# Raw attention slabs split inside each attention, logits turned, opening by tiles, one head's scores a slot later

## The reference

```python
x = x + 0.5 * ffn(layernorm(x))
x = x + attn(layernorm(x))
x = x + 0.5 * ffn(layernorm(x))
```

## Time and profile before

| what | value |
|---|---|
| median of three executions | 1925.19 us (1920.02 to 1925.96) |
| the profiled execution, its own time | 1923.59 us |
| its span, first to last instruction | 1921.9 us |
| PE busy | 1871.7 us (97%) |
| DVE busy | 781.9 us (41%) |
| ACT busy | 507.0 us (26%) |
| POOL busy | 134.1 us (7%) |
| granted TensorE clock, mean | 0.996 of 2.4 GHz |

### The profile page before, as it was taken

How to read it: one execution, slowest core, us unless ns; L and a number is a source line. 1 busy time by engine, 2 the same in 40 slices (tenths; PEclk the granted TensorE clock), 3 DMA queues, 4 the chain that set the end, 5 groups by cost and what they waited for, 6 DMA issues and landing times.

```text
span 1921.9 us, 23031 instructions
## 1 busy us (share of the span) xinstructions
PE 1871.7 (97%) x9024; PEld 1564.9 (81%) x9024; DVE 781.9 (41%) x1464; ACT 507.0 (26%) x780; POOL 134.1 (7%) x231
## 2 busy tenths in 40 slices
PE   4899999999999999999999999999999999999998
PEld 3778787888888888888888888888888888888887
DVE  4456644454343454323424455343454323423222
ACT  2333421343213332111311343213332111311111
POOL 0012110010000100000001010000100000000000
PEclk9899999999999999999999999999999999999999
DMA  4798876555575644576567564575644576567664
GB/s 146 250 352 330 296 285 255 191 191 170 174 249 186 211 165 165 193 242 230 203 222 271 192 216 171 170 249 186 211 165 165 195 245 233 198 220 253 222 238 162
DMA packets 95099, 416.38 MB, mean 217 GB/s; under 512 B 11760, under 2 KB 12144, under 8 KB 67984
## 3 DMA queue, kind: packets, MB, share of 16 engines
q1 hardware_dynamic: 56416, 291.29, 42.6%
q0 software_dynamic: 12336, 77.34, 10.3%
q10 hardware_dynamic: 26240, 46.28, 8.9%
HBM read 365.71 MB, written 49.15 MB: 216 GB/s over the span
## 4 chain that ended last, share of the span: by engine, by line
PE 91%; DVE 3%; ACT 2%; DMA 2%; issue 1%; SPq 1%; ACTq 0%; DVEq 0%
PE bank L932 26%; PE bank L934 26%; PE bank L933 26%; PE bank L1153 4%; PE bank L942 1%; PE bank L964 1%; PE bank L963 1%; PE bank L1082 1%; PE bank L1096 1%; DMA wt<-scr_w 1%; PE bank L1095 1%; PE bank L1088 1%; DMA b_all<-wgu 1%; DVE act_t L608 1%; PE bank L987 0%
## 5 line engine op out<-in xcount | busy, mean ns | idle before, releaser
L932 PE MATMUL bank<-x_hi,wt 128*128 128x512 f32 x1408 | 558.2, 396 | 4.1 <-DMA wt<-scr_w 2.7
L934 PE MATMUL bank<-x_lo,wt 128*128 128x512 f32 x1408 | 550.8, 391 | 0.0
L933 PE MATMUL bank<-x_hi,wt 128*128 128x512 f32 x1408 | 550.4, 391 | 0.0
L608 DVE TENSOR_TENSOR act_t<-bank,sig 128x512 f32<-128x512 f32 x176 | 121.6, 691 | 645.7 <-PE bank L1153 636.5
L932 PEld LDWEIGHTS bank<-x_hi,wt 128*128 128x128 f32 x1408 | 265.8, 189 | 57.5 <-DMA wt<-scr_w 3.6
L934 PEld LDWEIGHTS bank<-x_lo,wt 128*128 128x128 f32 x1408 | 265.3, 188 | 57.1
L933 PEld LDWEIGHTS bank<-x_hi,wt 128*128 128x128 f32 x1408 | 265.7, 189 | 52.3
L932 PE MATMUL bank<-dt,a_hi 128*128 128x512 f32 x704 | 279.5, 397 | 0.3 <-DVE a_lo L608 0.3
L934 PE MATMUL bank<-dt,a_hi 128*128 128x512 f32 x704 | 275.1, 391 | 0.0
L933 PE MATMUL bank<-dt,a_lo 128*128 128x512 f32 x704 | 274.3, 390 | 0.0
L561 ACT ACTIVATE sig<-bank 128x512 f32<-128x512 f32 x176 | 105.3, 598 | 503.2 <-PE bank L1153 503.2
(11 more groups left out here) (166 smaller groups left out, 1752.0 us busy)
## 6 DMA issues: line engine op xcount, KB each, us to landing
wt<-scr_w SPq DMA_DIRECT2D x154, 1152.0 KB, 5.2
dt<-scr_d SPq DMA_DIRECT2D x154, 512.0 KB, 5.2
s_bc<-scr_s ACTq DMA_DIRECT2D x128, 256.0 KB, 5.3
tw<-scr_t POOLq DMA_DIRECT2D x28, 1024.0 KB, 5.3
scr_w<-wt POOLq DMA_DIRECT2D x22, 1152.0 KB, 8.4
b_all<-wgu SPq DMA_DIRECT2D x22, 512.0 KB, 7.6
scr_d<-dt POOLq DMA_DIRECT2D x22, 512.0 KB, 6.1
scr_t<-tw POOLq DMA_DIRECT2D x7, 1024.0 KB, 7.7
```

The lines of the kernel that those rows point to most:

```text
L608: return nc.vector.tensor_tensor(dst, a, b, op)
L932: mm(dst, wh, xh, start=start, stop=False)
L933: mm(dst, wl, xh, start=False, stop=False)
L934: return mm(dst, wh, xl, start=False, stop=stop)
```

## The change

It removes the scratch copy of the attention slabs (scr_t, store_t, raw_slab, the splits in phase 0). Each attention now loads the raw slab (512 KB, POOL's queue) into raw_t, which becomes the state tile, and ACT and DVE split it in the slots of SPLIT. PE waits for the split (t_lo_ok) where it waited for the load. Besides: the logits are made the other way round (gate_s stationary, 512 tokens moving: 8 matmuls), copied whole by ACT into lgT, and four small matmuls with fold_m add the halves and turn them back, at k = 39; the maximum and exp move to k = 39 and 40. The scores of head 0 move from k = 31 to 32, its state update from 32 to 33. Block 0 is loaded in four tiles on SP, the constants on ACT's queue with semaphores of their own; the weights of the decays are split after step 1. The last down product of a phase signals each tile (y_ok), and flush takes them one by one.

```diff
-        scr_t = nc.dram_tensor("scr_t", (SLABS, P, 2 * GW), F32, kind="Internal").ap()
+        fold_m = sb("fold_m", [P, E])
-        raw_t = k_all[:, 2:4, :].rearrange("p a b -> p (a b)")
+        raw_t = st_flat[:, 0:GW]
+        lgT = tb_flat[:, 3 * NT * E + NT * 2 * P + NB:3 * NT * E + NT * 2 * P + 2 * NB]
+        def step_of(k):
+            return {31: 5, 32: 1, 33: 2}.get(k, (k - 30) % 6)
+        SPLIT = {4: S_V, 9: S_G, 16: S_QK, 22: S_QK + 1, 24: S_QK + 2, 26: S_QK + 3, 28: S_WO}
...
# SP
-            sp.dma_start(xr(0), x_t[0]).then_inc(ld_x[0], 16)
-            sp.dma_start(ident[:], c_id).then_inc(ld_const, 16)
...
+            for i in range(NT):
+                sp.dma_start(xr(0)[:, i, :], x_t[0][:, i, :]).then_inc(ld_x0[i], 16)
             raw(0)
             sp.dma_start(mask.rearrange("p a b -> p (a b)"), c_mask).then_inc(ld_mask, 16)
             raw(1)
...
-                if c % 2 == 0 and c // 2 - 1 < SLABS:
-                    raw_slab(c // 2 - 1)
# POOL
             def load_t(t, s):
-                slot, fill = slab_at(t, s)
-                pool.dma_start(tw[:, slot, :].bitcast(F32), scr_t[s]).then_inc(t_in[slot], 16)
+                n = t * SLABS + s
+                if n:
+                    pool.wait_ge(t_lo_ok, n)
+                pool.dma_start(raw_t, wat[s]).then_inc(raw_t_in, 16)
...
                 if t == 0:
-                    for i in range(2):
-                        pool.wait_ge(st_t[i], 16 * (SLABS // 2 + (i == 0)))
+                    pool.wait_ge(decay_ok, 1)
                 else:
-                    pool.wait_ge(wo_ok, t * NT)
+                    pool.wait_ge(o_ok, t * H)
                 load_t(t, S_V)
...
                 rstd_of(LN_T[t])
...
+                for n in range(S_G, S_QK + 2):
+                    load_t(t, n)
                 pool.wait_ge(gt_ok, 2 * t + 2)
...
+                for n in range(S_QK + 2, SLABS):
+                    load_t(t, n)
# ACT
-            def t_hi(s):
-                act.wait_ge(raw_t_in, 16 * (s + 1))
-                wait(act, st_t[s % 2], 16 * (s // 2))
-                copy(tw[:, s % 2, 0:GW], raw_t).then_inc(t_hi_ok, 1)
+            def t_hi(t, s):
+                n = t * SLABS + s
+                act.wait_ge(raw_t_in, 16 * (n + 1))
+                if s >= S_QK + 2:
+                    act.wait_ge(k_mm, t * H + s - S_QK - 1)
+                elif s == S_QK + 1:
+                    act.wait_ge(g_mm, 2 * t + 2)
+                elif s == S_QK:
+                    act.wait_ge(v_mm, 2 * t + 2)
+                elif s == S_V:
+                    wait(act, k_mm, t * H)
+                elif t:
+                    act.wait_ge(wo_ok, t * NT)
+                copy(tw[:, n % 2, 0:GW], raw_t).then_inc(t_hi_ok, 1)
...
-                    copy(r_a, W1[:].rearrange("p (t c) -> p t c", t=NT)[:, :, 0:E]).then_inc(logit_cp, 1)
-                elif k == 39:
+                    copy(lgT, W1[:]).then_inc(logit_cp, 1)
+                elif k == 40:
...
+            act.dma_start(ident[:], c_id).then_inc(ld_id, 16)
+            act.dma_start(raw_gate, w_gate).then_inc(ld_gate, 16)
...
+            router(0, 32)
+            router(0, 33)
+            act.wait_ge(ld_gate, 16)
+            copy(gate_s[:, :, 0:E], raw_gate).then_inc(gate_hi_ok, 1)
...
             gu_hi(0)
-            for k in range(32, 37):
+            gu_hi(1)
+            act.dma_start(raw_k1, w_gk1).then_inc(ld_const, 16)
+            for r in range(6):
+                act.dma_start(raw_k2[r * LOW:(r + 1) * LOW, :], w_gk2).then_inc(ld_const, 16)
+            act.dma_start(reset[:], c_reset).then_inc(ld_const, 16)
+            act.dma_start(bias[:], bgk).then_inc(ld_const, 16)
+            act.dma_start(wn[:], wnorm.partition_broadcast(P)).then_inc(ld_const, 16)
+            for k in range(37, 43):
                 router(0, k)
...
+                    if n == 1:
+                        decay_weights()
# DVE
-                elif k == 38:
-                    dve.wait_ge(logit_cp, p + 1)
-                    step(tt(r_a, W1[:].rearrange("p (t c) -> p t c", t=NT)[:, :, E:2 * E], r_a, ALU.add))
-                    step(nc.vector.tensor_reduce(mx, r_a, AX.X, ALU.max))
+                elif k == 39:
+                    dve.wait_ge(folded, p + 1)
...
+                    step(nc.vector.tensor_reduce(mx, logits, AX.X, ALU.max))
...
             def attention(t, k, q):
                 r, s, xb = LN_T[t], (q + 1) % 2, xr(t)
+                if k in SPLIT:
+                    t_lo(t, SPLIT[k])
...
                 for i in range(NT):
+                    if i + 1 < NT:
+                        dve.wait_ge(y_ok, p * (NT - 1) + i + 1)
+                    else:
+                        dve.wait_ge(d_used, (p + 1) * CH)
                     nc.vector.scalar_tensor_tensor(xb[:, i, :], YB[i][:], 0.5, xb[:, i, :], ALU.mult, ALU.add).then_inc(x_ok, 1)
...
+            first_stats(0)
+            first_stats(1)
+            norm(LN_R[0], 0, xr(0))
+            first_stats(2)
+            norm(LN_R[0], 1, xr(0))
+            first_stats(3)
...
             m_mask(0)
+            router(0, 43)
+            router(0, 44)
             m_rest(0)
# PE
                 elif k == 38:
                     pe.wait_ge(x_lo_ok, (r + 1) * NT)
-                    for i in range(NT):
-                        for kk in range(KC):
-                            mm(W1[:, cols(i)], x_hi[:, s, kk, cols(i)], gate_s[:, kk, :], start=(kk == 0), stop=False)
-                            ins = mm(W1[:, cols(i)], x_lo[:, s, kk, cols(i)], gate_s[:, kk, :], start=False, stop=(kk == KC - 1))
+                    for kk in range(KC):
+                        mm(W1[:], gate_s[:, kk, :], x_hi[:, s, kk, :], start=(kk == 0), stop=False)
+                        ins = mm(W1[:], gate_s[:, kk, :], x_lo[:, s, kk, :], start=False, stop=(kk == KC - 1))
                     ins.then_inc(logit_ok, 1)
+                elif k == 39:
+                    pe.wait_ge(logit_cp, p + 1)
+                    for i in range(NT):
+                        ins = mm(W1[:, cols(i, E)], lgT[:, cols(i)], fold_m[:], start=True, stop=True)
+                    ins.then_inc(folded, 1)
...
-                    h, m = (k - 30) // 6, (k - 30) % 6
+                    h, m = (k - 30) // 6, step_of(k)
...
-            pe.wait_ge(ld_const, 16 * N_CONST)
+            pe.wait_ge(ld_id, 16)
             for k in range(32, 37):
                 router(0, k)
+            pe.wait_ge(gate_ok, 1)
+            router(0, 38)
             pe.wait_ge(setup_lo, 2)
             masked(0)
+            pe.wait_ge(fold_ok, 1)
+            router(0, 39)
             main(GB, 0, 0, 0)
             main(UB, P, 0, 0)
```

More of the change, by code:

```diff
@@ L187, in build @@
         out_t = out.rearrange("(b t p) d -> b p t d", p=P, t=NT)
[L188 removed]
+        N_CONST = 10
         def wait(eng, s, v):
@@ L230, in raw @@
                 sp.dma_start(raw_d[:, half, :], wdn[half, j]).then_inc(raw_d_in[half], 16)
-            def raw_slab(s):
-                wait(sp, t_lo_ok, s)
-                sp.dma_start(raw_t, wat[s]).then_inc(raw_t_in, 16)
             def load_w(p, c):
@@ L370, in _ @@
                 store_d(c)
-                if c % 2 == 1 and c // 2 - 1 in range(SLABS):
-                    store_t(c // 2 - 1)
                 if c == 8:
@@ L577, in _ @@
             gu_hi(0)
-            for k in range(32, 37):
+            gu_hi(1)
[6 more added lines that the diff above has]
+            for k in range(37, 43):
                 router(0, k)
-            gu_hi(1)
             m_top(0)
-            for k in range(37, SLOTS):
+            for k in range(43, SLOTS):
                 router(0, k)
@@ L876, in rest_a, with decay_rests, first_stats @@
                 tt(a_lo[:, n % 2, :], act_t[:], a_hi[:, n % 2, :].bitcast(F32), ALU.subtract).then_inc(a_lo_ok, 1)
-            dve.wait_ge(ld_x[0], 16)
-            dve.wait_ge(pool_init, 1)
-            router(0, 28)
-            dve.wait_ge(ld_const, 16 * N_CONST)
+            def decay_rests():
+                dve.wait_ge(decay_hi, 1)
+                k1v = k1_s[:].rearrange("p k (r a e) -> p k r a e", r=4, a=2)
+                tt(k1v[:, :, :, 1, :], raw_k1.unsqueeze(2).broadcast_to([P, KC, 4, LOW]), k1v[:, :, :, 0, :].bitcast(F32), ALU.subtract)
+                rows = slice(4 * LOW, 6 * LOW)
+                tt(gk2_s[rows, :], raw_k2[rows, :], gk2_s[rows, :].bitcast(F32), ALU.subtract).then_inc(decay_ok, 1)
+            def first_stats(i):
+                dve.wait_ge(ld_x0[i], 16)
+                stats_of(LN_R[0], i, xr(0))
+            first_stats(0)
[5 more added lines that the diff above has]
+            for i in range(NT):
+                low(LN_R[0], i, 0, YB[i])
+                if i < 2:
+                    norm(LN_R[0], i + 2, xr(0))
+                if i == 2:
+                    dve.wait_ge(gate_hi_ok, 1)
```

(26 more changed lines are left out.)

124 lines of the change are left out of this document (51 added, 73 removed).

## The result

The changed kernel takes **1887.65 us** in the median of five runs (1886.59 to 1890.33), the kernel before 1922.25 in five (1918.04 to 1925.96). The ratio is 0.982, with an interval from 0.980 to 0.984: 34.6 us less. I had forecast 1893.1, from 1883 to 1905, so the sign and the range held, and the gain was 4.1 us more than the 30.5 of the sum. (The other 1.3 between forecast and median is that the sum starts at a profiled execution of 1923.59.) The profiled execution took 1890.33 with a span of 1888.6, against the span of 1921.9 before: 33.3 less.

The account below looks back on a forecast made before the run. PE, busy for 97% of the span, was taken to bound the kernel. Terms -11.7 - 4.5 - 5.5 - 2.7 - 4.3 - 1.8 = -30.5 took 1923.6 to 1893.1 us, range 1883 to 1905.

Parts of the forecast that it names:

- Opening: Start of phase 0: PE needs only tile 0, its norm and ident, so line 1153 starts earlier; -11.7 us, bounds -8 and -14.5.
- rival B: The opening gives back through ACT's ten issues, a late tile 0 and the half clock: about 1902 us, chance 0.15.
- Turned logits: Logits on PE in seven warm phases: 8 matmuls and a fold replace 32 matmuls; -4.5 us, bounds -9 to +1.
- Splits leave phase 0: Phase 0: PE's waits for masked weights behind slab splits go, with the half clock after; -5.5 us, bounds -8.5 and -2.
- Start of phase 1: First wt loads of phase 1: fewer slab bytes queued ahead, both PE waits go; -2.7 us, bounds 0 and -3.
- Scores: Attentions: scores one slot later, so four PE waits before them go, with the restart; -4.3 us, bounds 0 and -4.5.
- Splits in the attentions: 28 more splits on ACT and DVE, hidden in slots where these wait for PE; 0 us, bounds 0 and +10.
- rival E: Last three slab loads of an attention chain through splits; landings above 12 us cost time, up to 1961 us; chance 0.03.
- End: End of the kernel: three of four additions overlap the last matmuls; -1.8 us, bounds -1 and -2.2.
- A: The forecast itself, whole kernel: 1893 us, own range 1885 to 1901, chance 0.66.
- C: Slabs land a little late in each attention, ACT stands at the split, 3 us four times: 1905 us, chance 0.07.
- D: Phase 0's waits after router work go too, 2.9, and the fold is cheap, 4: 1886 us, chance 0.05.

Follow-up runs that it names:

- e1: The kernel before with the turned logits alone: 1911.37 us in one run.
- e3: The changed kernel with the scratch copy back (slabs split in phase 0, stored and loaded as 1 MB): 1894.42 us in the median of four runs.
- e7: The changed kernel with block 0 loaded in one transfer again, all statistics behind it: 1887.90 us in one run.
- v1: The changed kernel with the norm of the next router's first tile two slots earlier in phases with an attention: 1884.22 us in two runs.
- e4: The changed kernel with every split of a slab done twice on ACT and DVE: 1892.21 us in one run.
- e5: The changed kernel with every slab loaded two or three times, one load after the other: 1896.31 us with two loads, 1949.19 with three.
- e8: The changed kernel with the additions at a phase's end waiting for the whole down product again: 1889.40 us in two runs.
- e9: The changed kernel unaltered, measured once more: 1887.06 us in the median of four runs.

## Why the prediction held, point by point

- **Opening**, booked -11.7, measured -15.3, just beyond its bound of -14.5. The step that failed is "ten DMA issues that stand in its program ahead of the logit copy ... so 5.4: 21.5". The order was right and the price near (4.6); the start was wrong, since the issues began at 13.2, beside the slab copies, and not behind them at 16.1. The copy stood at 17.88, the maximum at 20.18 and not at 23.1, 2.9 earlier. A further 1.3 came from the clock: the 24 matmuls after the fold start 0.23 apart, where I had booked 6.7 us, and the 0.4 for m_rest did not show. That makes the 4.7 by which line 1203 (36.94) is ahead of my 41.6; step 1 gave 1.1 back. I had also forgotten that the masked product of step 0 stands between the logits and the fold and keeps PE at work (17.41 to 19.12), so the gap by which rival B lived was not there. The rule that I had drawn on for it, that PE's throttled clock is the default and activity releases it (the Trainium skill, "TensorE: Matmul & The Clock Gate", Part 1), was not put to the test: PE idles 0.78 before the fold in e1 and 1.08 in e3, and the matmuls behind it start 0.23 apart in both, but no run has the 2 us that rival B named. PE's first instruction (6.54 for 7.0) and the logits (13.86 for 13.7) came as booked. How the 15.3 divide is shown only in part: undoing the tiles costs 0.8 to 2.6 at line 1203 (e7), and the turned logits alone, in the kernel before, gave 4.2 (e1). That the larger part of the rest is the constants, for which nothing waits any more, is read from PE's first instruction (18.2 and 6.54) and was not tried by itself.
- **Turned logits**, -4.5 booked, -5.3 measured: by the pairs the fold costs 0.95, not 1.04, and the logits got 1.71 shorter, not 1.68.
- **Splits leave phase 0**, -5.5 booked, 6.1 by undoing it (e3), -6.8 in the two traces. Four waits went, in steps 5, 9, 11 and 15: 2.01, 0.67, 0.34 and 0.77, 3.8 for the 4.0 booked. The term that was too small is what stands behind them, restarts and the half clock: 3.0 in the two traces for 1.6.
- **Start of phase 1**, -2.7 booked, -3.3 measured, and the reason was wrong. "POOL's queue had put the loads of two slabs, 2 MB, before it" is what the row showed, but e1 and e3 have these loads and no wait. The number was right because the profile of before held one late store.
- **Scores**, -4.3 booked, -3.0 measured. I had asked what is late next for the scores and the state, not for the transposes of the other work in those slots. v1 shows that the missing 1.3 and as much again were there, once the norm is moved as well.
- **Splits in the attentions**, 0 and 0, with room for twice the work (e4) and twice the landing (e5) everywhere but in step 3 of phase 4, which lost 1.5 and 7.1. The bound of rival E, 12 us for a chained landing, lies between the 7.6 to 10.3 of two loads, which cost those steps nothing, and the 13.5 of three, which cost 35.5. But "the tightest is the third of Q and K" was wrong: for PE the first slab of the third attention is. (For ACT the last slab is: in the first attention it lands 3.71 after its issue and is split 0.03 later, at no cost to PE.) The rule against this part, that DVE in a two-port mode, as in an fp32 copy, keeps GpSimd from writing the descriptors of the transfers that it issues (the Trainium skill, "SBUF — State Buffer", the box on the DVE that blocks DMA), did not show: the 28 loads took 5.4 in the median (3.6 to 9.9), where the loads of 1 MB took 5.3 by the same list of the page, and no issue of theirs on POOL took over 0.63. I had stretched the rule to every DVE instruction: DVE's part of a split is a TENSOR_TENSOR and no copy, and no trace here shows in which mode DVE ran, so this case does not test it.
- **End**, -1.8 booked, 2.0 by e8 and e9, hidden in five of eleven profiles by the late last store.
- **Rivals.** A held. B did not happen, E only with the loads made three times as long; C's late slabs cost one step of one attention with two loads. D's 1886 is nearer to 1887.65 than my 1893.1, but by luck: the waits behind router work, which it took away, are all still there (0.71, 1.38 and 0.21 in steps 10, 14 and 16, before and after), and the logits with their fold gave 0.8 more and not 4.

By the pairs of the two profiles the sum lacked 2.8 (33.3 for 30.5): 3.6 in the opening, 1.3 in phase 0, 0.8 in the logits and 0.6 in phase 1 too little, 1.3 in the scores, 1.8 at the end and 0.3 in phase 4 too much. So the small miss of the whole is in part errors that cancel. By the medians it lacked 4.1.

## What to carry to other kernels

Here DMA issues on ACT cost what stands behind them in its program about half a microsecond each, and what stands before nothing: put them behind long work whose successor has to wait anyway. When a wait is taken away by moving a step, look for what the engines do next in the same slots, since the wait may have covered it; moving one norm two slots up gave back 2.6, more than the 1.3 that the part had missed. And a wait that ends on a store or a load, seen in one execution, may be that execution's alone.

## What was not expected of the hardware

- Kernels that are alike in the opening run it in two forms 1.6 us apart, by whether the half clock falls ahead of a wait or behind it. What decides between them stays open; e8, v1 and e5 with three loads do not differ from the changed kernel there at all.
- In the opening, matmuls of 512 columns start 0.43 apart and those of 128 columns 0.21 apart (0.11 in a warm phase) while the granted clock of that stretch is printed as 1.00. The first clock record of the trace stands only at 19.2 (37.7 before), where the pitch falls; ahead of it the pitch and not that column tells the speed. In the kernel before, the narrow ones stayed so for 6.5 us; in e1 the wide ones were at 0.23 after 1.2 us, and in the changed kernel they stayed at 0.43 for 3.6 us. So width alone does not decide it.
- A store of the same size landed in 5.4 or in 8.3 us at the end of phase 0, and in 2.1 or 3.8 to 4.2 at the end of the kernel.
- Ten DMA issues of one engine ran ahead of the compute instructions that stand before them in its program.
